# Convolution, router and top-2 mixture of experts on one core: gate products that begin with the high part, an early list of 18 tiles from six chunks, paddings of list B moved, opening reordered

## What is computed

```python
x = x + relu(conv3x3_grouped(layernorm_c(x), kernel) + bias)     # 8 groups, padding SAME
t = tokens(x)                                                    # 4096 x 128
z = layernorm(t)
logits = z @ router_w.T                                          # 8 experts
top, idx = top_k(logits, 2); w = softmax(top)
y_e = (silu(z @ w_gate[e]) * (z @ w_up[e])) @ w_down[e]          # 128 -> 256 -> 128
out = t + sum over the token's two experts of w * y_e
```

## Time and profile before

| | us |
|---|---|
| median of 3 runs (lowest, highest) | 233.39 (232.08, 235.12) |
| the profiled execution, its own time | 234.28 |
| its span from first to last instruction | 232.3 |
| PE busy with products | 199.5 |
| DVE, POOL, ACT busy | 128.1, 125.9, 113.1 |
| mean granted TensorE clock, share of full speed | 0.941 |

### The profile page before, as it was taken

How to read it: one execution, slowest core, us unless ns; L and a number is a source line. 1 busy time by engine, 2 the same in 40 slices (tenths; PEclk the granted TensorE clock), 3 DMA queues, 4 the chain that set the end, 5 groups by cost and what they waited for, 6 DMA issues and landing times.

```text
span 232.3 us, 4516 instructions
## 1 busy us (share of the span) xinstructions
PE 199.5 (86%) x1186; PEld 165.4 (71%) x1186; DVE 128.1 (55%) x468; ACT 113.1 (49%) x251; POOL 125.9 (54%) x143
## 2 busy tenths in 40 slices
PE   7699989699999839797299999999999999999700
PEld 7466878589988637575288888888888888888500
DVE  5252687764787976667235555555555555555400
ACT  2477655335554113543145565655566565556200
POOL 6403025981776468066556665654257777666630
PEclk9999999859999985999979999999999999999955
DMA  6999300110111054017863444644132555521100
GB/s 190 383 389 375 100 1 13 35 38 12 45 33 46 25 142 108 15 35 222 202 181 112 126 120 106 169 135 144 48 100 73 160 151 154 154 78 44 45 24 0
DMA packets 22263, 26.34 MB, mean 113 GB/s; under 512 B 4176, under 2 KB 16980, under 8 KB 22240
## 3 DMA queue, kind: packets, MB, share of 16 engines
q1 hardware_dynamic: 17888, 17.46, 26.4%
q0 software_dynamic: 4064, 8.60, 10.9%
q10 hardware_dynamic: 288, 0.01, 0.1%
HBM read 15.84 MB, written 11.41 MB: 117 GB/s over the span
## 4 chain that ended last, share of the span: by engine, by line
PE 69%; DVE 10%; POOL 4%; issue 4%; SPq 3%; ACT 3%; DMA 1%; POOLq 1%; DVEq 0%
PE ps_y L443 13%; PE ps_gu L341 11%; PE ps_gu L417 10%; PE ps_gu L425 7%; PE ps_gu L422 7%; PE ps_h L433 7%; PE ps_z L405 4%; PE ps_y L307 3%; POOL out L1049 2%; PE ps_gu L321 1%; DMA zt<-zsa 1%; SPq L291 1%; DVE bn L683 1%; SPq L289 1%; PE ps_gu L357 1%
## 5 line engine op out<-in xcount | busy, mean ns | idle before, releaser
L1036 POOL DMA_INDIRECT zsb<-zt x38 | 37.0, 974 | 28.8 <-DMA zsb<-zt 13.2
L585 ACT ACTIVATE sg<-ps_gu,zt 128x256 f32<-128x256 f32 x76 | 36.1, 475 | 26.1 <-PE ps_gu L425 22.0
L1027 POOL DMA_INDIRECT zsa<-zr x32 | 31.9, 996 | 27.2 <-DVE zr L785 9.2
L341 PE MATMUL ps_gu<-pad,ckw 128*128 128x256 f32 x192 | 45.8, 394 | 0.0
L1049 POOL DMA_INDIRECT out<-zt x38 | 36.9, 972 | 16.0 <-issue 9.5
L443 PEld LDWEIGHTS ps_y<-wall,hT 128*128 128x128 f32 x304 | 39.5, 191 | 6.6 <-issue 3.4
L896 DVE TENSOR_TENSOR hh<-ps_gu,sg 128x512 f32<-128x512 f32 x38 | 26.3, 691 | 31.8 <-ACT sg L585 31.8
L443 PE MATMUL ps_y<-wall,hT 128*128 x304 | 40.3, 275 | 2.3 <-DVE zr L776 1.5
L341 PEld LDWEIGHTS ps_gu<-pad,ckw 128*128 128x128 f32 x192 | 37.1, 197 | 6.8 <-issue 1.4
L417 PE MATMUL ps_gu<-wall,z_lo 128*128 x76 | 38.1, 502 | 3.3 <-DVE z_lo L888 2.4
L904 DVE SCALAR_TENSOR_TENSOR zt<-ps_y,zt 128x128 f32<-128x128 f32 x76 | 23.1, 346 | 21.9 <-PE ps_y L443 21.9
(11 more groups left out here) (157 smaller groups left out, 214.9 us busy)
## 6 DMA issues: line engine op xcount, KB each, us to landing
zt<-zsb SPq DMA_DIRECT2D x38, 131.0 KB
zt<-zsa SPq DMA_DIRECT2D x38, 67.0 KB
xt<-x_rows SPq DMA_DIRECT2D x8, 256.0 KB, 7.4
ew<-gate_up_w SPq DMA_DIRECT2D x8, 256.0 KB, 6.7
xp<-x_pairs SPq DMA_DIRECT2D x8, 256.0 KB, 8.0
zsb<-nulls SPq DMA_DIRECT2D x8, 131.0 KB, 4.2
wall<-down_w SPq DMA_DIRECT2D x1, 1024.0 KB, 11.7
ckw<-conv_k SPq DMA_DIRECT2D x1, 768.0 KB, 6.0
```

The costliest lines, as they stand in the source:

```text
L341: last = nc.tensor.matmul(dst, ckw[:, h * BANDS + k, :], pad[n % 2][:, h * IMG:(h + 1) * IMG, below:below + PAIRS, dx:dx + WW], start=k == ...
L585: nc.scalar.activation(sg[u % 2][:, s, :], ps_gu[u % 2][:, s * N:s * N + H], ACT.Silu, scale=zt[:, u % RING, s, RSTD:RSTD + 1]).then_inc(s ...
L1027: nc.gpsimd.indirect_dma_start(zsa, bass.IndirectOffsetOnAxis(zr[:, i, SLOT_A:SLOT_A + 1].bitcast(U32), 0), zr[:, i, :], None, bounds_chec ...
L1036: nc.gpsimd.indirect_dma_start(zsb, bass.IndirectOffsetOnAxis(row[:, SLOT_B:SLOT_B + 1].bitcast(U32), 0), row, None, bounds_check=last_row ...
```

## The change

- `EARLY` goes from 4 to 5: the early list has 18 tiles (9 units) and needs six chunks scattered; 38 units stay. Since the ring has 8 buffers, the ninth early unit's load (unit 8) now waits for unit 0's store, ahead of the paddings on SP.
- `gate_up` begins with z_hi times the high part, then z_hi times the residual, and ends with z_lo times the high part. The wait for z_lo stands before the last product.
- SP's opening order: the convolution's weights before the expert weights, x(2) and x(3) earlier. The paddings of list B (`zsb`) come after the loads of four units of list A's later part.
- PE, ACT, DVE in the opening: chunk 0 is normalised and padded first; expert weights 1 to 7 later.
- DVE per chunk: `residual(n, 1)` in its own chunk, ahead of `order_pair(n - 1)` (before, in the next chunk's turn); statistics and shifts of later groups earlier; `early_table` after `slots(5)`; `early_row` after `top_two(6)`; `z_tails(0)` ahead of `slots(6)`.
- DVE at the end of the chunks: the integer copy of the regions' ends inside `slots(7)`; `full_counts` and `full_table` one unit earlier.
- ACT per chunk: `weigh(n - 2)` before `pad_both(n + 1)`. PE: the early table's transposes after `conv(7, 1)`. POOL: the rstd of x groups 3 and 4 before the first scatter.

```diff
-EARLY = 4
+EARLY = 5
...
             load_x(0)
             load_x(1)
+            sp.dma_start(ckw[:], conv_k).then_inc(ck_loaded, 16)
             load_gate_up(0)
             load_gate_up(1)
-            sp.dma_start(ckw[:], conv_k).then_inc(ck_loaded, 16)
             load_xp(0)
+            load_x(2)
             load_gate_up(2)
-            load_x(2)
...
-            for e in range(1, E):
-                sp.dma_start(zsb[bass.ds(ends_at[E + e], P), :], nulls[:]).then_inc(b_padded, 16)
             for n in range(BATCHES[EARLY][1], CHUNKS):
                 sp.wait_ge(scattered[n], 16 * TT)
             sp.wait_ge(null_tiles, 32)
             sp.wait_ge(a_padded, 16 * (E - 1))
             sp.wait_ge(table_ready, 2)
-            load_set(U1, U2, zsa, ROW_A, tab2, 2 * TILES)
+            load_set(U1, U1 + 4, zsa, ROW_A, tab2, 2 * TILES)
+            for e in range(1, E):
+                sp.dma_start(zsb[bass.ds(ends_at[E + e], P), :], nulls[:]).then_inc(b_padded, 16)
+            load_set(U1 + 4, U2, zsa, ROW_A, tab2, 2 * TILES + 8)
...
                 if s == 0:
                     pe.wait_ge(z_hi_ready, u + 1)
-                    pe.wait_ge(z_lo_ready, u + 1)
...
-                nc.tensor.matmul(dst, z_lo[u % 2][:, s, :], hi, start=True, stop=False)
+                nc.tensor.matmul(dst, z_hi[u % 2][:, s, :], hi, start=True, stop=False)
...
-                nc.tensor.matmul(dst, z_hi[u % 2][:, s, :], hi, start=False, stop=False)
+                nc.tensor.matmul(dst, z_hi[u % 2][:, s, :], lo, start=False, stop=False)
...
-                nc.tensor.matmul(dst, z_hi[u % 2][:, s, :], lo, start=False, stop=True).then_inc(gu_ready, 1)
+                if s == 0:
+                    pe.wait_ge(z_lo_ready, u + 1)
+                nc.tensor.matmul(dst, z_lo[u % 2][:, s, :], hi, start=False, stop=True).then_inc(gu_ready, 1)
...
             for n in range(CHUNKS):
-                if n >= 1:
-                    residual(n - 1, 1)
...
                 residual(n, 0)
...
                 if n >= 2:
                     slots(n - 2)
                     write_weights(n - 2)
                 if n == CHUNKS - 1:
-                    early_row()
+                    early_table()
                 if n >= 1:
                     stats_t(n - 1)
                     variance_t(n - 1)
-                    top_two(n - 1)
                     if n == CHUNKS - 1:
                         residual(n, 1)
+                    top_two(n - 1)
+                    if n < CHUNKS - 1:
+                        residual(n, 1)
+                    else:
+                        early_row()
                     order_pair(n - 1)
                     scale_gap(n - 1)
...
+            z_tails(0)
             slots(LAST - 1)
             stats_t(CHUNKS - 1)
             variance_t(LAST)
             write_weights(LAST - 1)
-            z_tails(0)
             top_two(LAST)
```

More of the change, by code:

```diff
@@ L232, in _ @@
             load_x(1)
+            sp.dma_start(ckw[:], conv_k).then_inc(ck_loaded, 16)
             load_gate_up(0)
             load_gate_up(1)
-            sp.dma_start(ckw[:], conv_k).then_inc(ck_loaded, 16)
             load_xp(0)
+            load_x(2)
             load_gate_up(2)
-            load_x(2)
             load_gate_up(3)
+            load_x(3)
             load_gate_up(4)
+            load_gate_up(5)
             load_xp(1)
-            load_gate_up(5)
-            load_x(3)
             load_gate_up(6)
@@ L453, in _ @@
             transpose_x(0)
-            for e in range(1, 4):
-                centre(e)
+            centre(1)
             pe.wait_ge(ck_loaded, 16)
@@ L469, in _ @@
                 if n == 0:
-                    centre(4)
-                    centre(5)
+                    centre(2)
+                    centre(3)
+                conv(n, 1)
                 if n == CHUNKS - 1:
@@ L475, in _ @@
                     table(0, entry1, 2, T1)
-                conv(n, 1)
                 if n == 0:
-                    centre(6)
-                    centre(7)
+                    for e in range(4, E):
+                        centre(e)
             rows_and_logits(CHUNKS - 1)
@@ L602, in _ @@
             pad_both(0)
+            router_blocks()
             normalise_x(1)
-            for e in range(1, 4):
-                weight_heads(e)
+            weight_heads(0)
             act.wait_ge(bias_loaded, 16)
             add_bias(0)
+            weight_heads(1)
             for n in range(CHUNKS):
+                if n >= 2:
+                    weigh(n - 2)
                 if n + 1 < CHUNKS:
                     pad_both(n + 1)
-                if n >= 2:
-                    weigh(n - 2)
+                if n == 0:
+                    weight_heads(2)
+                    weight_heads(3)
                 if n >= 1:
@@ L768, in slots @@
                 nc.vector.tensor_tensor(base[:, b, :], ranks[:, c, :], start, ALU.add).then_inc(base_ready, 1)
+                if b == LAST:
+                    dve.wait_ge(base_ready, LAST + 1)
+                    nc.vector.tensor_copy(base_i[:], base[0:1, LAST, :]).then_inc(regions_ready, 1)
                 dve.wait_ge(slot_step, 3 * b + 1)
@@ L927, in _ @@
             nc.vector.tensor_copy(upper[:], upper_f[:]).then_inc(upper_ready, 1)
-            weight_tails(0)
             shift_x(1)
@@ L931, in _ @@
             pad_odd_of_first()
-            for e in range(1, 4):
-                weight_tails(e)
+            weight_tails(0)
             stats_x(2)
+            weight_tails(1)
             stats_x(3)
@@ L940, in _ @@
             for n in range(CHUNKS):
-                if n >= 1:
-                    residual(n - 1, 1)
+                if n == 1:
+                    residual(0, 1)
+                if n == 2:
+                    shift_x(3)
+                if n == 3:
+                    shift_x(4)
+                if 1 <= n <= 2:
+                    stats_x(2 * n + 2)
+                    stats_x(2 * n + 3)
+                    variance_x(n + 2)
+                residual(n, 0)
                 if n == 0:
                     shift_x(2)
-                if n == 2:
-                    shift_x(3)
-                if n == 4:
-                    shift_x(4)
-                if n == CHUNKS - 1:
-                    early_table()
-                residual(n, 0)
+                    for e in range(2, E):
+                        weight_tails(e)
                 if n >= 2:
@@ L959, in _ @@
                     variance_t(n - 1)
-                    top_two(n - 1)
                     if n == CHUNKS - 1:
                         residual(n, 1)
+                    top_two(n - 1)
[3 more added lines that the diff above has]
+                        early_row()
                     order_pair(n - 1)
                     scale_gap(n - 1)
-                if n == 0:
-                    for e in range(4, E):
-                        weight_tails(e)
-                if 1 <= n <= 2:
-                    stats_x(2 * n + 2)
-                    stats_x(2 * n + 3)
-                    variance_x(n + 2)
+            z_tails(0)
             slots(LAST - 1)
@@ L995, in _ @@
                     write_weights(LAST)
+                    full_counts()
                 if u == 3:
-                    full_counts()
-                if u == 4:
                     full_table()
@@ L1091, in _ @@
             pool.wait_ge(ids_ready, 1)
+            rstd_x(3)
             half_rstd_t(0)
-            rstd_x(3)
+            rstd_x(4)
             for n in range(CHUNKS - 1):
```

5 lines of the change are left out of this document (removed).

## The result

The changed kernel takes 224.27 us (median of 4 runs, 223.66 to 225.76) against 234.25 (232.08 to 237.69, 4 runs) for the kernel before: ratio 0.961, 95% interval 0.953 to 0.969. Some executions of either kernel take a few per cent longer than its others, so every ratio here compares the faster ones alone, in which the kernel before took 231.7 to 235.2 us. The profiled execution of the changed kernel took 225.76 us, its slowest, with a span of 223.8, so 8.5 us less than the profiled execution of before. The forecast was 10.1 less.

A forecast was written before the change was run, and what follows sets the result against it. PE was taken to bound the list stage, with waits and half clock ahead of it; 1.8 + 6.6 - 3.4 - 0.8 + 3.5 - 1.3 + 3.7 = 10.1 us off 234.28 gave 224.2, median 223.3, range 219 to 229.

The forecast's parts named there:

- The list stage, per unit: Gate products on PE: z_hi first removes the whole 0.18 us lost per unit, period 3.14 to 2.96.
- Rival 1: List stage: weight load stays uncovered or something else holds the first product, only 0.07 a unit; 225.1 us, chance 0.17.
- The opening: Chunk 0 normalised and padded first: first convolution at about 11.1 against 14.5, lead 1.8 us.
- The chunks: PE's waits of 1.05 and 2.29 us for DVE's residual and the half clock go: 6.6, lead 8.4 at chunk 7.
- Rival 4: Chunks: rank's mask comes late behind the residual on DVE, PE waits at half clock; 239 us, chance 0.03.
- The early list: Unit 0 waits for chunk 5's scatter: first gate product 81.9 against 86.94, -3.4; z_tails(0) order costs 0.8, lead 4.2 after.
- two units more before the stall, its own shift: Term of the sum at list A's later part: +3.5 us, PE restarting with unit 9 instead of unit 7.
- The stall: List A's later part: SP's waits, paddings, table and load let PE go on at 116.2 with unit 9, lead 7.7 us.
- The half clock behind the stall: PE at unit 9 after the stall: turn 4.44 against 3.14, costing 1.3 us, lead 6.4 from unit 10.
- Rival 3: Unit 8's wait is longer and the half clock after the stall lasts twice as long, 3.4 more; 228.7 us, chance 0.15.
- POOL's chain: Stores of units 16 to 18, each behind the last's landing, don't shrink; with 2.6 us to spare POOL ends 10.1 earlier.
- The ring: Late list stage: unit 28's load waits for unit 20's store, up to 1.6 us of PE waiting, lead 9.7 to 11.3.

The follow-up runs named there:

- experiment 1: The kernel before with only the new order of gate products (z_lo times high last, its wait at the third); 229.27 us, ratio 0.986.
- experiment 2: The changed kernel with the gate products back in the old order (z_lo first); 230.50 us, ratio 0.990 to the kernel before.
- experiment 6: The changed kernel with DVE's old order in the chunks and POOL's two reciprocal roots of x where they stood; 230.76 us, ratio 0.986.
- experiment 5: The changed kernel with EARLY back at 4 (early list of 14 tiles, 7 units); 217.67 us, ratio 0.934 to the kernel before.
- experiment 3: The changed kernel with SP's load of unit 8 behind list A's seven paddings instead of ahead; 219.18 us, ratio 0.943 to the kernel before.
- experiment 8: The changed kernel with POOL looking for stores later (unit u - 2 for list A's last two units too); 224.28 us, ratio 0.962.
- experiment 7: The changed kernel with z_tails(0) moved back behind write_weights(6) on DVE; 224.04 us, ratio 0.959 to the kernel before.
- experiment 9: The changed kernel with list B's paddings again ahead of the loads of list A's later part; 225.60 us, ratio 0.968.
- experiment 10: The changed kernel with EARLY = 4, z_tails(0) behind write_weights(6), list B's paddings spread behind loads of units 11 to 17, POOL's reports four units back; 216.53 us, ratio 0.926.
- experiment 11: As experiment 10, plus the early table one chunk earlier and the full table one unit earlier, on DVE and PE; 214.41 us, ratio 0.919.
- experiment 4: As experiment 3, plus the full table one unit earlier on PE and DVE; 219.23 us, ratio 0.942 to the kernel before.

## Why the prediction was right, and where its steps were off

The time was forecast at 223.3 and came out at 224.27, faster by more than the measurement's uncertainty, inside the range of 219 to 229. The profiled execution was 1.6 off, the median only 1.0, because that execution was the slowest, 1.5 above the median, where 0.9 had been taken. Step by step:

- **The list stage, per unit.** Forecast 2.96, measured 2.95 to 2.96, in the changed kernel and alone in experiment 1. Rival 1 is refuted: the five products around the change from unit to unit start 0.23 to 0.24 apart, each with its load of 0.19 under the one before. The rule of the Trainium skill ("TensorE: Matmul & The Clock Gate", Part 3) that was weighed against it does not hold for these products. The margin of 0.16 for z_hi is what the trace has: 147.42 plus 0.18 is 147.60, PE could begin at 147.76. Not forecast: in the stretch at half clock around unit 0 the new order saves about 1 us more (units 0 and 1 3.17 apart for 4.20, experiment 1 against the kernel before; the waits in experiment 2).
- **The opening.** First convolution at 10.92 (11.1 forecast), lead 1.8 as forecast.
- **The chunks.** The lead at chunk 6's rows is 8.7 against 8.4, and experiment 6 gives the term back (6.9 between chunks 0 and 6, 6.6 forecast). Rival 4 did not come: the clock is full until 75.5.
- **The early list.** Scatter 69.44 and 74.36 (69.4 and 74.3 forecast), first gate product 81.65 (81.9), PE still for 5.35. Right, and `z_tails(0)` cost 0.6 for 0.8. What this step did not see is that the edit had no return beside the others. The sum sets +3.5 for "two units more before the stall, its own shift" against 3.4 and 0.8. Experiment 5 shows that with 14 tiles the stall would have shrunk by itself, because paddings, table and chunk 7's scatter had moved up as well: unit 9 comes 6.0 earlier with the short list, and 4.0 earlier with the long list and the paddings ahead of unit 8's load (experiment 3). The sum was right for the change as a whole, and the price of this part was not in it.
- **The stall.** Forecast 116.2 for unit 9, measured 117.25. Unit 0's store landed earlier than taken (103.7, not 105.0), the ends' load took 0.4 more, but the seven paddings took 4.61 for 3.65, and the last needed 2.9 until SP could go on for 1.6. The mechanism was right, as experiment 3 shows: with the paddings ahead of that wait, issued from 94.87 on, the stall is 1.25 in place of 5.72.
- **The half clock behind the stall** is the term that was most off: 1.3 us forecast, from the one case of before; measured 5.60 from unit 9 to unit 10, so 2.65. Rival 3's second half happened, the half clock lasting 6.8 us, at a price of 1.35 more in place of 3.4. Over the runs this number is loose, and the traces show what it goes by: not the idle time before, but how much of the stretch at half clock is left when PE restarts. The unit's turn is longer by 0.41 to 0.48 of that.

| run | idle before | clock at half for | of it behind the restart | first turn longer by |
|---|---|---|---|---|
| before (unit 7) | 4.45 | 3.4 | 3.1 | 1.30 |
| experiment 1 (unit 7) | 4.76 | 3.4 | 3.4 | 1.62 |
| changed kernel (unit 9) | 5.72 | 6.8 | 6.0 | 2.65 |
| experiment 2 (unit 9) | 4.17 | 6.8 | 6.1 | 2.47 |
| experiment 8 (unit 9) | 5.41 | 6.8 | 4.7 | 2.22 |
| experiment 6 (unit 9) | 5.41 | 6.8 | 4.0 | 1.89 |
| experiment 7 (unit 9) | 5.75 | 3.4 | 2.9 | 1.41 |
| experiment 9 (unit 9) | 7.00 | 6.8 | 3.0 | 1.42 |
| experiment 10 (unit 7) | 1.92 | 3.4 | 3.4 | 1.63 |
| experiment 11 (unit 5) | 1.88 | 3.4 | 3.4 | 1.63 |

  After 1.25 us of idle (experiment 3) and 1.96 (experiment 5) the clock stayed full, and the turns were 3.34 and 3.25; after 1.92 and 1.88 it fell.
- **POOL's chain.** It kept its length in the changed kernel (unit 16's row to the first store into the output: 16.2 us before, 16.0 after; the other versions with the same reports have 14.8 to 16.4) and gave the 2.6 us of room back, so that from 5.8 the lead grew to 8.5. But the forecast took 1.2 off for it, and it costs 0.6 (experiment 8). The ring never held PE here: unit 31's load landed 0.18 before its transpose, the closest that the trace tells. In experiments 1 and 5 it did, for 0.18 and 0.26.

Sum over the errors: unit 9 1.1 later and its half clock 1.2 more; 0.6 back, because the row of unit 16, on which POOL's chain hangs, is made three turns behind its transpose, each 0.19 shorter, which the step left out; 0.1 in the rest. That is 1.6, the distance between 10.1 and 8.5.

What stays open: why the clock falls sooner or later into about the same idle time and stays at half for 3.4 or 6.8 us, why seven paddings take longer behind unit 8's load than elsewhere, and what holds the last 1.9 us before the table in experiment 11 together (rank, slots and table are one chain of PE and DVE that was not taken apart).

## What to carry to other kernels

A queue in program order is a chain of its own: one new wait on it (unit 8's load for unit 0's store) holds everything behind, here seven paddings that could have gone out eleven microseconds earlier (94.87 against 106.08), and moving it was worth 5 us. When several parts of a change move the same stall, price each with the others already in place: two more units of work ahead of the stall came out even in a sum over the old kernel (-3.4 and +3.5; no run shows them there alone), and beside the other parts they cost 6.6 us, of which SP's order alone gives 5.1 back. And a wait removed shows what was late next: after unit 9 came unit 13, after the loads the tables.

## What the runs showed of the hardware

- A stretch of half clock behind a stall of 4.2 to 7 us cost 1.3 to 2.65 us over a normal unit in eight traces: 0.41 to 0.48 of the part of the stretch that lay behind PE's restart. Two traces with 1.92 and 1.96 us of idle before the same unit differ in whether the clock fell at all (experiments 10 and 5). One profile is not enough to price it.
- Seven equal DMAs issued in a row by SP took 3.49 us in the kernel before and in experiments 1, 3, 4, 5, 10 and 11. In the changed kernel and experiments 2, 6, 7, 8 and 9, where they follow unit 8's load, they took 4.05 to 4.95: one of the last three issues took 0.9 to 1.8 there, and all others 0.33 to 0.37. POOL's DMAs went out beside them in both groups, so their presence alone is not the difference; the cause is not shown. In the changed kernel the last landed 4.4 after its issue began, against 2.0 for the quickest.
- After POOL's second store of unit 18 its next store went out 2.91 us behind that issue in twelve of thirteen traces (3.70 in experiment 8); after unit 17's it took 3.65 to 5.45 in the same twelve. An estimate of 2.3 us from the Trainium skill ("DMA: Bandwidth & Descriptors", Anatomy of one DMA) is below all of them. From unit 16's row to the first store into the output these twelve traces have 14.8 to 16.5 us.
